# The last key's p v products of an eight-key tile moved from GpSimd to ScalarE

## What is computed

```python
xn = _layernorm(x, axis=-1)
x = x + _L0_attn_ref(xn, Wqkv, bqkv, Wproj, bproj) + _L0_ffn_ref(xn, weight, bias)
...
qkv = x @ Wqkv.T + bqkv                 # 16 heads of 32
scores = mask + scale * jnp.einsum('bnd,bmd->bnm', q, k)
attn = jax.nn.softmax(scores, axis=-1)
out = jnp.einsum('bnm,bmd->bnd', attn, v)
out = out.transpose(1, 0, 2).reshape(n, b, ch)
return out @ Wproj.T + bproj
```

## Time and profile before

| what | value |
|---|---|
| three runs | 1547.1, 1547.19, 1548.22 us |
| the profiled execution | 1547.0 us, its span 1545.2 us |
| granted TensorE clock | 0.991 |
| TensorE busy | 1488.2 us (96%) |
| VectorE busy | 1463.4 us (95%) |
| GpSimd busy | 1372.8 us (89%) |
| ScalarE busy | 1036.8 us (67%) |
| L461, GpSimd's products | 699.5 us, 192 of them |
| L974, VectorE's sum over keys | 429.0 us, 128 of them |

### The profile page before, as it was taken

How to read it: one execution, slowest core, us unless ns; L and a number is a source line. 1 busy time by engine, 2 the same in 40 slices (tenths; PEclk the granted TensorE clock), 3 DMA queues, 4 the chain that set the end, 5 groups by cost and what they waited for, 6 DMA issues and landing times. The chain is left out here.

```text
span 1545.2 us, 22934 instructions
## 1 busy us (share of the span) xinstructions
PE 1488.2 (96%) x6749; PEld 674.9 (44%) x6872; DVE 1463.4 (95%) x1220; ACT 1036.8 (67%) x1995; POOL 1372.8 (89%) x1035
## 2 busy tenths in 40 slices
PE   6999999999999999999999999999999999999955
PEld 3444444444444444444444444444444444444422
DVE  6999999999999999999999999999999999999997
ACT  5676666767667676766677776676766767766532
POOL 2589999999899989989998999999989998998985
PEclk9999999999999999999999999999999999999979
DMA  7444554545445454554545455554644545454333
GB/s 223 89 106 100 129 117 113 130 114 135 110 117 132 110 131 115 123 121 121 123 108 137 111 126 123 111 132 112 135 113 117 129 114 125 119 124 111 90 76 108
DMA packets 368685, 184.53 MB, mean 119 GB/s; under 512 B 316336, under 2 KB 316336, under 8 KB 368560
## 3 DMA queue, kind: packets, MB, share of 16 engines
q1 hardware_dynamic: 368560, 183.06, 49.7%
HBM read 73.41 MB, written 33.55 MB: 69 GB/s over the span
## 5 line engine op out<-in xcount | busy, mean ns | idle before, releaser
L461 POOL TENSOR_TENSOR prod_pv<-kv,probs 128x2048 f32<-128x2048 f32 x192 | 699.5, 3644 | 9.9
L974 DVE TENSOR_REDUCE o_nat<-prod_pv 128x512 f32<-128x2048 f32 (+1 forms) x128 | 429.0, 3352 | 40.9 <-POOL prod_pv L461 23.3
L865 DVE TENSOR_REDUCE scores<-prod_qk 128x64 f32<-128x2048 f32 x192 | 439.3, 2288 | 6.8 <-DVE prod_qk L860 0.2
L860 DVE TENSOR_TENSOR prod_qk<-q_ps,kv 128x1536 f32<-128x1536 f32 (+1 forms) x192 | 398.0, 2073 | 0.2 <-issue 0.2
L701 PE MATMUL k_ps<-wqkv_hi,xT 128*128 128x512 f16 x1024 | 327.1, 381 | 5.4 <-DMA xT<-x 4.9
L701 PE MATMUL proj_ps<-wproj_hi,oT 128*128 128x512 f16 x1008 | 323.5, 382 | 6.8 <-ACT proj_ps L554 6.8
L701 PE MATMUL v_ps<-wqkv_hi,xT 128*128 128x512 f16 x1024 | 325.7, 379 | 0.0
L701 PE MATMUL q_ps<-wqkv_hi,xT 128*128 128x512 f16 x1024 | 325.7, 379 | 0.0
L651 ACT ACTIVATE kv<-v_ps 128x512 f32<-128x512 f32 x128 | 142.3, 1112 | 151.4 <-PE v_ps L701 151.4
L701 PE MATMUL k_ps<-wqkv_lo,xT 128*128 128x512 f16 x512 | 195.3, 381 | 0.0
L701 PE MATMUL v_ps<-wqkv_lo,xT 128*128 128x512 f16 x512 | 194.3, 380 | 0.0
(11 more groups left out here) (117 smaller groups left out, 1852.3 us busy)
## 6 DMA issues: line engine op xcount, KB each, us to landing
xn<-in_L_attn_x SPq DMA_DIRECT2D x128, 256.0 KB, 2.8
xs<-in_L_attn_x SPq DMA_DIRECT2D x128, 256.0 KB, 2.6
out<-xs SPq DMA_DIRECT2D x128, 256.0 KB, 2.1
xT<-x SPq DMA_TRANSPOSE x256, 3.0
kv<-in_L_attn_Wqkv SPq DMA_DIRECT2D x3, 1024.0 KB, 8.2
oT<-o SPq DMA_TRANSPOSE x128, 3.2
kv<-in_L_attn_Wproj SPq DMA_DIRECT2D x1, 1024.0 KB, 5.8
prod_pv<-in_L_ffn_weight SPq DMA_DIRECT2D x1, 1024.0 KB, 9.5
```

Source lines behind the costliest of these rows:

```text
L461: nc.gpsimd.tensor_tensor(o, v, p, ALU.mult).then_inc(pv_multiplied, 1)
L860: nc.vector.tensor_tensor(prod_qk[:, 1:1 + m0 + 4 - m1, :], qb, k, ALU.mult).then_inc(qk_multiplied, 1)
L865: nc.vector.tensor_reduce(scores[:, n % 2, :, m0:m0 + 4].rearrange("p h m -> p m h"), prod_qk[:, row:row + 4, :].rearrange("p m (h d) -> p ...
L974: nc.vector.tensor_reduce(o_nat[:, n % 2, :], prod_pv[:, place:place + units, :].rearrange("p q (c m) -> p c q m", m=4), AX_XY, ALU.add).t ...
```

## The change

In an eight-key tile the second unit of products (keys 4 to 7) loses key 7 on GpSimd: three keys, 1536 elements. ScalarE makes the products of key 7, one head at a time, as 16 activations of 128 x 32 with the probability of that head as the scale, which is a pointer to one number per partition. It reads every eighth fp32 of `v_all` and writes every fourth of `prod_pv`. Heads 0 to 7 come just ahead of the copy of k, heads 8 to 15 between the preset of the k bank and the copy of v, in slot n + 11. ScalarE waits for `probs_ready`, `v_kept` and `pv_summed` there; VectorE's sum (L974) and GpSimd's `probs` of the tile two on wait for the new semaphore `last_key_multiplied`.

```diff
@@ probabilities (GpSimd)
                 after(pool, pv_multiplied, unit_count(i, last_unit(n - 2)))
+                after(pool, last_key_multiplied, heavy_count(i, n - 2))
@@ products (GpSimd)
                 o = prod_pv[:, u % PRODS, :].rearrange("p (h d m) -> p h d m", d=D, m=4)
+                if m0:
+
+                    v, p, o = v[:, :, :, 0:3], p[:, :, :, 0:3], o[:, :, :, 0:3]
@@ ScalarE
+            def last_key_products(i, n, first, last):
+
+                u = key_units(n)[1][0]
+                after(act, probs_ready, tile_count(i, n))
+                after(act, v_kept, tile_count(i, N * (n // N) + N - 1))
+                after(act, pv_summed, unit_count(i, u - PRODS))
+                for h in range(first, last):
+                    step = nc.scalar.activation(prod_pv[:, u % PRODS, :].rearrange("p (c m) -> p c m", m=4)[:, h * D:(h + 1) * D, 3],
+                                                v_all[:, (n // N) % 2, h * D:(h + 1) * D, N - 1], ACT.Copy,
+                                                scale=probs[:, n % 2, h, N - 1:N])
+                if last == H:
+                    step.then_inc(last_key_multiplied, 1)
@@ slot (ScalarE)
                     linear_into_bank(i, j)
+                if live(i, j, L_PV) and keys_of(j - L_PV) == N:
+                    last_key_products(i, j - L_PV, 0, H // 2)
                 if live(i, j, L_KV):
...
                     preset_k()
+                if live(i, j, L_PV) and keys_of(j - L_PV) == N:
+                    last_key_products(i, j - L_PV, H // 2, H)
@@ slot (VectorE), ahead of the sum over keys
                     after(dve, pv_multiplied, unit_count(i, last_unit(n)))
+                    if units == 2:
+                        after(dve, last_key_multiplied, heavy_count(i, n))
```

More of the change, by code:

```diff
@@ L272, in attention_and_fp8_linear @@
         pv_multiplied = sem("pv_multiplied")
+        last_key_multiplied = sem("last_key_multiplied")
         pv_summed = sem("pv_summed")
```

## The result

The changed kernel takes 1538.61 us (median of five runs, 1538.02 to 1539.59), the kernel before 1547.19 in the same comparison (1547.04 to 1548.71). The ratio is 0.9943, with a 95% interval of 0.9928 to 0.9957: 8.6 us faster. The profiled execution has a span of 1536.2 us against 1545.2. The prediction said 1535.5, in 1531 to 1549.

The account below looks back on a forecast made before the run. A loop of VectorE and GpSimd was taken to set 91.8 us a period, TensorE hardly behind at 91.5. Terms of -4.5, -0.9, -5.2, -1.3 and +0.2 made -11.7: 1547.0 to 1535.3, median 1535.5, range 1531 to 1549.

Parts of the forecast that it names:

- The forecast case: VectorE's wait for GpSimd goes, its lead grows until ScalarE's last key holds it: 1535.5 us, chance 0.49.
- TensorE's waits, slots 22 to 126: TensorE's short waits for the transposed x go, as GpSimd is earlier: -4.5 us.
- the same, slots 15 to 22: Of 1.9 us TensorE lost there, the later half goes after the first shortened GpSimd units: -0.9 us.
- VectorE's lead over TensorE: VectorE runs ahead, up to 1.4 us a period, until it stands at ScalarE's new semaphore: -5.2 us.
- the end, with the added waits: GpSimd's last four units end before VectorE's subtraction, shortening it: -1.3 us; added queue waits at the end: +0.2 us.
- GpSimd's part: The second unit, 512 elements fewer, falls from 3.64 to 2.78 us; VectorE's 1.67 us wait for GpSimd just goes.
- The price of a product: One ScalarE product of 128 x 32, called c, takes 0.24 us: 3.8 a tile, 246 for all 64 tiles.
- Rival 3: ScalarE becomes the bound from c = 0.34, TensorE waiting for x; 1570 us at c = 0.37; chance 0.13.
- Rivals 1 and 2: 1: only TensorE's waits go, 1541 us, chance 0.16. 2: three keys cost GpSimd as much as four, 1547, 0.18.

Follow-up runs that it names:

- the saving given back: Changed kernel plus two GpSimd products of 128 x 128 into an unused tile ahead of the second unit of each eight-key tile: 1547.26 us.
- twice the saving: Changed kernel with GpSimd making two keys instead of three in the second unit, key 6 left out: 1538.78 us.
- products early: Changed kernel with all 16 ScalarE products directly after the projection's result, ahead of the linear's copies, nothing left out: 1535.71 us.

## Why the prediction was right

The forecast case came, with its mechanism, and its sum was 2.7 us too large. Term by term, from the profiled executions, in which the span fell by 9.0:

| term | predicted | measured | how read |
|---|---|---|---|
| TensorE's waits, slots 22 to 126 | -4.5 | -4.6 | 1189.68 for 1194.24 |
| the same, slots 15 to 22 | -0.9 | -0.8 | 81.2 for 82.0 |
| VectorE's lead over TensorE | -5.2 | -3.3 | lag in slot 131: 10.45 for 13.78 |
| the end, with the added waits | -1.1 | -0.2 | from that sum to the end: 93.46 for 93.64 |

- **GpSimd's part** was right: 2.80 for 2.78. That the wait goes, "just", also: with the saving given back it returns, with twice the saving nothing more comes.
- **The price of a product** was right in size (0.242 for 0.24) and half wrong in its working: I put the surcharge on the write, after the copy of v, and it belongs to the read. The write's price in the earlier trace rows and the read's happen to be nearly equal, so that the number came out is in part luck. Why the copy of v holds the engine for so long (it steps by 32 bytes, not 16, and reads another memory) stays open.
- **The lead** is the term that was mis-sized. "Counted from the exp of slot 63" I had the last key at 697.0 + 64c, with c = 0.242 at 712.5, 9.3 us after slot 66's first matmul. It ended at 10.2. I had let ScalarE run from that exp without a wait. But the projection's result and the two copies of the linear stand ahead of the products, and TensorE's linear can be read only 3.9 us after its slot begins. ScalarE's timeline of the first heavy slot of the period, slot 119, which TensorE opens at 1306.50, has the two waits:

```profile
1309.51 0.69 ACT L649 ACTIVATE projected<-proj_ps,out_scale 128x512 f32<-128x512 f32 x1 [0.66 <-PE proj_ps L723]
1310.37 0.60 ACT L547 ACTIVATE linear<-lin_ps 128x512 f16<-128x512 f32 x1 [0.17 <-PE lin_ps L742]
```

  The last heavy slot, 122, which TensorE opens at 1340.82, has none:

```profile
1339.55 1.09 ACT L673 ACTIVATE kv<-v_ps 128x512 f32<-128x512 f32 x1
...
1344.69 0.60 ACT L547 ACTIVATE linear<-lin_ps 128x512 f16<-128x512 f32 x1
1345.32 0.69 ACT L559 ACTIVATE proj_ps<-linear,out_unscale 128x512 f32<-128x512 f16 x1
1345.95 2.04 ACT L569 ACTIVATE prod_pv<-kv,probs 128x32 f32<-128x32 f32 x8
1347.88 0.58 ACT L660 ACTIVATE kv<-k_ps 128x512 f32<-128x512 f32 x1
1348.50 0.60 ACT L541 ACTIVATE k_ps<-k_bias 128x512 f32<-128x512 f32 x1
1349.03 2.03 ACT L569 ACTIVATE prod_pv<-kv,probs 128x32 f32<-128x32 f32 x8
1350.97 1.08 ACT L673 ACTIVATE kv<-v_ps 128x512 f32<-128x512 f32 x1
```

  The first product starts 5.1 us into slot 119 and into slot 122 (1345.95 - 1340.82); for the first heavy slot I had 4.0. From one copy of v to the next are 11.42 us without a wait, for TensorE's 11.44 (I had 7.65 + 16c, it is 7.55 + 16c), so what the first heavy slot starts with stays through all four. The late start, less what the shorter slots give back, is 0.9 of the missing 1.9 us. Another 0.2 lies between the last key and the start of the sum, and 0.6 is my choice of slot 67 as the reference for before: the lag was 14.4 there and 13.8 in the last period. The rest is rounding. The two variants that move only the products confirm this reading: ahead of the linear 7.6, ahead of the projection's result 6.3.
- **The end** was the other miss. The subtraction that I named did fall from 1.97 to 0.69 us, and one that I had not named from 1.81 to 0.82. The one between them, which took 2.02 before, took 4.04 (next section but one): 2.3 us gained and 2.0 lost.
- **Rival 3** did not come at c = 0.242, but its point was put too high: "from c = 0.34 on" ScalarE would make TensorE wait for x. TensorE does wait for x there in the runs with 8 and 4 more products, but what sets the period is a loop of ScalarE and VectorE through the q banks, 96.4 us with 24 products and 92.5 with 20. Four tiles of 16 instead of 24 products take 4 x 8 x 0.242 = 7.7 less: 88.7 us for the changed kernel against TensorE's 91.5. By this estimate the room is 2.8 us a period, 0.044 a product, and the break point is at 0.286. By the same loop, c = 0.37 gives 88.7 + 64 x 0.128 = 96.9 us a period, where the run with 24 products had 96.4 and took 1616.8 us: the 1570 that I gave for it was far too low.
- **Rivals 1 and 2** are out: the lag shrank, and three keys cost three quarters of four.

## What to carry to other kernels

When engines follow written-out orders and one of them sets the pace, a moved step is priced by the moment at which its last result comes, measured from the pacing engine's slot, and not by its busy time: 250 us of new work on ScalarE cost nothing, and moving it 4 us within the slot was worth another 4 us. So place it behind the earliest point at which its inputs are there, and ahead of steps whose results are asked for a slot later. And before new work is put on an engine, follow each loop that closes through it (here ScalarE, VectorE and the q banks): the shortest slack of those loops, by the estimate above 2.8 us in 91.5, is the room, not the idle share of 33%.

## What the runs showed of the hardware

**VectorE's subtraction waits for GpSimd's running instruction.** At the end of the span VectorE subtracts two SBUF operands (L902) while GpSimd makes products. The timelines of VectorE and GpSimd of the changed kernel:

```profile
1510.56 4.04 DVE L902 TENSOR_TENSOR o<-o_nat,o 128x512 f16<-128x512 f32 x1 [1.37 <-ACT o L624]
```

```profile
1510.42 3.63 POOL L466 TENSOR_TENSOR prod_pv<-kv,probs 128x2048 f32<-128x2048 f32 x1
```

GpSimd's instruction ends at 1514.05, the subtraction at 1514.60, 0.55 later. In the twelve other profiled executions of this study the second such subtraction also ended 0.55 us after the end of the GpSimd instruction that was running when it started, and took from 2.01 to 4.04 us by how much of that was left; with GpSimd idle it takes 0.69 us. So GpSimd sets its end. Counted from the sum in slot 131 it ends at 71.82 us in the changed kernel, and at the same 71.82 with the products early, where it starts 1.1 us later and takes 2.92. In the kernel before it was 70.72. That is what took most of the gain at the end back. The page GPSIMD Engine Reference of the Trainium skill (Key points) says that GpSimd shares its SBUF interfaces with VectorE, with contention for VectorE's instructions with two SBUF inputs; these rows agree, and show how long it lasts here.

**A pointer as scale and a short row.** A product of 128 x 32 has a length of 0.34 us and holds ScalarE for 0.240 to 0.250 from one start to the next, each time in the changed kernel; 16 in a row, in the variant with the products early, take 4.0 us.
